# Cross-attention on Trainium2: score products in two row strips, value products in blocks of four

## What is computed

```python
# layer 0: RMS norms on x and ctx; layer 1: biases, boolean mask (all False here), layer norm
q, k, v = x @ Wq.T + bq, ctx @ Wk.T + bk, ctx @ Wv.T + bv        # (8, 100 or 1444, 128)
scores = einsum('bqhd,bkhd->bhqk', heads(q), heads(k)) / sqrt(8)
attn = softmax(scores, axis=-1)
o = einsum('bhqk,bkhd->bqhd', attn, heads(v))
# layer 0, 1: x = norm(x + o @ Wo.T + bo) (layer 0 without the outer norm); layer 3: x = norm(x + o)
# layer 2: the same with causal scores, then gelu(x @ W1.T + b1) @ W2.T + b2 + x
```

## Time and profile before

| | us |
|---|---|
| median of 3 runs | 1240.93 |
| lowest, highest | 1237.69, 1241.09 |
| profiled execution | 1242.44 |
| its span | 1240.6 |
| TensorE busy | 1059.6 (85%) |
| VectorE busy | 857.3 (69%) |
| ScalarE busy | 825.3 (67%) |
| GpSimd busy | 372.6 (30%) |
| mean granted TensorE clock | 0.96 of 2.4 GHz |

### The profile page before, as it was taken

The page is one execution under the profiler, slowest core; times in us unless marked ns, Lnnn a source line. Parts: engine busy times, 40 slices in busy tenths (PEclk is TensorE's granted clock), DMA queues, the critical chain, the costliest instruction groups (busy, mean ns, idle before and its releaser), DMA issues.

```text
span 1240.6 us, 30123 instructions
## 1 busy us (share of the span) xinstructions
PE 1059.6 (85%) x9938; PEld 638.9 (51%) x9938; DVE 857.3 (69%) x1757; ACT 825.3 (67%) x1788; POOL 372.6 (30%) x339
## 2 busy tenths in 40 slices
PE   1469888888998999988998889998999989998886
PEld 0245445445555555655555555565556556565442
DVE  5678678578766766875876657576777858777650
ACT  1237756667776777776777676657677766767565
POOL 6744433344411311330231413232242413323000
PEclk9979999899999999998999999799999999999898
DMA  7212212212221221221232120202021121201100
GB/s 187 62 37 58 61 27 58 58 30 60 65 58 33 73 74 32 72 79 38 58 77 52 39 71 21 55 24 58 22 62 35 48 61 28 61 24 31 35 3 4
DMA packets 57587, 62.92 MB, mean 51 GB/s; under 512 B 16826, under 2 KB 50906, under 8 KB 57302
## 3 DMA queue, kind: packets, MB, share of 16 engines
q1 hardware_dynamic: 57430, 60.89, 19.0%
HBM read 23.63 MB, written 0.41 MB: 19 GB/s over the span
## 4 chain that ended last, share of the span: by engine, by line
PE 58%; DVE 16%; issue 10%; ACT 10%; SPq 3%; DMA 1%; POOL 1%; DVEq 0%; ACTq 0%; POOLq 0%
PE sexp L700 15%; PE acc L719 14%; PE smax L664 12%; DVE mx L1096 7%; ACT probs L965 5%; PE shared L616 3%; PE shared L604 3%; SPq L403 2%; DVE mneg L1102 2%; PE shared L593 2%; PE shared L784 2%; PE smax L676 1%; DVE qs L1083 1%; PE shared L626 1%; SPq L469 1%
## 5 line engine op out<-in xcount | busy, mean ns | idle before, releaser
L965 ACT ACTIVATE probs<-sexp 120x400 f32<-120x400 f32 (+1 forms) x1152 | 558.9, 511 | 237.9 <-PE sexp L700 226.6
L1096 DVE TENSOR_TENSOR mx<-smax,mx 120x400 f16<-120x400 f32 (+1 forms) x1056 | 557.2, 567 | 167.7 <-PE smax L664 161.4
L700 PE MATMUL sexp<-qexp,krep 97*120 97x400 f16 (+1 forms) x1152 | 403.8, 360 | 61.1 <-ACT probs L965 41.8
L664 PE MATMUL smax<-qmax,krep 96*120 96x400 f16 (+1 forms) x1152 | 367.3, 350 | 37.5 <-DVE mx L1096 29.1
L700 PEld LDWEIGHTS sexp<-qexp,krep 97*120 97x120 f16 (+1 forms) x1152 | 152.1, 136 | 216.7 <-ACT probs L965 144.6
L719 PE MATMUL acc<-probs,vx 120*18 120x200 f32 (+1 forms) x4608 | 262.1, 347 | 1.0 <-ACT probs L965 0.9
L664 PEld LDWEIGHTS smax<-qmax,krep 96*120 96x120 f16 (+1 forms) x1152 | 157.6, 138 | 92.6 <-DVE mx L1096 51.3
L488 POOL TENSOR_TENSOR ct<-ctf,ct 128x480 f16<-128x480 f32 (+1 forms) x72 | 82.8, 1151 | 346.2 <-ACT ct L902 346.2
L719 PEld LDWEIGHTS acc<-probs,vx 120*18 120x18 f32 (+1 forms) x4608 | 109.0, 99 | 114.8 <-issue 84.5
L1094 DVE CAST mx<-smax 121x400 f16<-121x400 f32 x96 | 51.3, 570 | 120.3 <-PE smax L664 120.2
L488 POOL TENSOR_TENSOR kp<-kf,kp 128x480 f16<-128x480 f32 (+1 forms) x72 | 79.2, 1106 | 114.6 <-ACT kp L916 114.6
(11 more groups left out here) (133 smaller groups left out, 994.0 us busy)
## 6 DMA issues: line engine op xcount, KB each, us to landing
nat<-in_ctx SPq DMA_DIRECT2D x24, 720.0 KB
krep<-kp SPq DMA_DIRECT2D x576, 30.0 KB, 1.9
krep<-kp SPq DMA_DIRECT2D x288, 30.2 KB, 1.9
qexp<-qmax SPq DMA_DIRECT2D x24, 300.0 KB, 3.4
maskexp<-maskmax SPq DMA_DIRECT2D x8, 281.2 KB, 3.4
anymask<-in_mask SPq DMA_DIRECT2D x1, 1128.1 KB, 6.7
mask<-in_mask SPq DMA_DIRECT2D x8, 141.0 KB
wq<-in_w_qkv SPq DMA_DIRECT2D x1, 768.0 KB
```

The lines of the kernel that those rows point to most:

```text
L664: last = pe.matmul(ps, krep[0:PARTS, u.par, t, c0:c0 + r], qmax[:, u.par, t, :, :].rearrange("p h s -> p (h s)"), start=True, stop=not masks)
L700: last = pe.matmul(ps, krep[:, u.par, t, c0:c0 + r], qexp[:, u.par, t, :, :].rearrange("p h s -> p (h s)"), start=True, stop=not masks)
L965: act.activation(probs[0:r, j % PR, :], sexp[j % SR][0:r, 0:QW], ACT.Exp).then_inc(sem["probs_ready"], 1)
L1096: op = dve.tensor_tensor(dst, src, dst, ALU.max)
```

## The change

Score products. `krep` and the new `qx` have two strips of 64 rows. A strip holds, for its half of the heads, 16 rows of keys three times (48 rows, `KROWS`), then a row of ones that meets the maximum row. A tile is now (chunk, pair of t, strip i) and its score product two products of 48 or 49 rows by 200 columns, a = 0 and 1, into the halves of one bank. Exp and maximum products are issued in turns, and maximum tiles run `LEAD = 13` tiles ahead of the step, so that the maximum tile of a step lies in the other strip than its exp tile; maximum tiles now fill all 48 steps, the first 13 of a unit in the stage before.

Queries. `qmax` and `qexp` become one tile `qx` with three buffers; there is no copy for the exponentials. The maximum row goes out as two DMAs. VectorE's correction of the low part covers all 128 rows.

Keys. `keep_keys` writes `kp` to HBM (3 DMAs a unit), `replicate` reads it back into `krep` in 6 DMAs a group instead of 12.

Value products. `TOGETHER = 2`: blocks of four products, each still over the four column groups.

Order. The maxima are transposed in the shared banks at steps 36 and 37 and `mn` is at 41. Stages are written out with constant semaphore values instead of loops. The two copies of the program behind the flag start at stage 6.

The diff, cut to its core:

```diff
-PARTS = 3 * 32
+PARTS = 128
+STRIP = 64
+KROWS = 48
-TOGETHER = 4
+TOGETHER = 2
 VALUES_AT = [j // TOGETHER * TOGETHER + TOGETHER + 1 for j in range(NSTEP)]
-MAX_AT = [i * 39 // NSTEP for i in range(NSTEP)]
-MT_AT = 39
+LEAD = 13
...
+        def tile_of(j):
+
+            return j // T, j // 2 % 2, j % 2
+
+        def max_tile(s, j):
+
+            u, i = (s.top, j + LEAD) if j + LEAD < NSTEP else (s.prep, j + LEAD - NSTEP)
+            return (u, i) if u is not None else None
...
             while n <= last:
-                b0 = units[n].batch if 0 <= n < len(units) else None
-                if b0 == 1 and n + 3 <= last:
-                    for i in range(2):
-                        await_read(engine, i)
-                    with engine.Fori(1, 4, 2) as b:
-                        enter_loop(n, units, b)
-                        run(stage_of(n, units, b, n), n)
-                        run(stage_of(n + 1, units, b, n), n)
-                        leave_loop(n, units, b)
-                    n += 4
-                else:
-                    run(stage_of(n, units), n)
-                    n += 1
+                run(stage_of(n, units), n)
+                n += 1
...
-        MASK_STAGES = B - 1, 2 * B - 1
+        MASK_STAGES = B - 2, 2 * B - 1
...
+            def keep_keys(u, g):
+
+                _, c0, n, _ = groups()[g]
+                sp.wait_ge(*at("k_lo", u, g + 1))
+                sp.wait_ge(*at(f"krep_in{g}", u, PER[f"krep_in{g}"][u.L] * -1))
+                sp.dma_start(kept[u.par, :, :, c0:c0 + n], kp[:, :, c0:c0 + n]).then_inc(sem[f"k_kept{g}"], 16)
...
-                for t in range(T):
+                for i in range(2):
                     for j, part in enumerate((0, 0, 1)):
-                        sp.dma_start(krep[32 * j:32 * j + 32, u.par, t, c0:c0 + n],
-                                     kp[32 * t:32 * t + 32, part, c0:c0 + n]).then_inc(sem[f"krep_in{g}"], 16)
+                        at_row = STRIP * i + 16 * j
+                        sp.dma_start(krep[at_row:at_row + 16, u.par, :, c0:c0 + n],
+                                     kept[u.par, :, part, c0:c0 + n].rearrange("(t i r) n -> i r t n", t=T, i=2)[i]
+                                     ).then_inc(sem[f"krep_in{g}"], 16)
...
+                    pe.wait_ge(*at("probs_ready", u, j - SR + 1))
+                at_row = STRIP * i
                 ps = sexp[j % SR][0:r, 0:QW]
-                last = pe.matmul(ps, krep[:, u.par, t, c0:c0 + r],
-                                 qexp[:, u.par, t, :, :].rearrange("p h s -> p (h s)"), start=True, stop=not masks)
+                last = pe.matmul(ps[:, 2 * S * a:2 * S * a + 2 * S],
+                                 krep[at_row:at_row + KROWS + 1, u.par, 2 * tp + a, c0:c0 + r],
+                                 qx[at_row:at_row + KROWS + 1, u.third, 2 * tp + a, :, :].rearrange("p f s -> p (f s)"),
+                                 start=(a == 0 or not masks), stop=not masks, skip_group_check=masks)
...
-                for p in range(2):
-                    q, slot = 2 * (t % 2) + p, t // 2
-                    last = pe.matmul(acc[32 * q:32 * q + VW, 2 * S * slot:2 * S * slot + 2 * S],
-                                     vx[0:r, u.par, PAIRS * c + 2 * t + p, :],
-                                     probs[0:r, j % PR, 2 * S * p:2 * S * p + 2 * S],
-                                     start=(c == 0 and slot == 0), stop=(c == NCH - 1), skip_group_check=True)
+                for a in range(2):
+                    q = 2 * a + i
+                    last = pe.matmul(acc[32 * q:32 * q + VW, 2 * S * tp:2 * S * tp + 2 * S],
+                                     vx[0:r, u.par, PAIRS * c + 2 * (2 * tp + a) + i, :],
+                                     probs[0:r, j % PR, 2 * S * a:2 * S * a + 2 * S],
+                                     start=(c == 0 and tp == 0), stop=(c == NCH - 1), skip_group_check=True)
...
             def stage(s, n, masks=False):
                 for j in range(NSTEP):
-                    if s.exp is not None:
-                        exp_scores(s.exp, j, masks and s.exp.L == 1)
-                    for i in range(NSTEP):
-                        if MAX_AT[i] == j and s.top is not None:
-                            max_scores(s.top, i, masks and s.top.L == 1)
+                    m = max_tile(s, j)
+                    for a in range(2):
+                        if s.exp is not None:
+                            exp_product(s.exp, j, a, masks and s.exp.L == 1)
+                        if m is not None:
+                            max_product(*m, a, masks and m[0].L == 1)
...
                         for i in range(3):
-                            act.wait_ge(*at(act, f"krep_in{i}", u, 0))
+                            act.wait_ge(*at(f"k_kept{i}", u, 0))
...
-                dve.tensor_tensor(qs[32:64, :, :], qf[32:64, :, :], qs[32:64, :, :], ALU.subtract
-                                  ).then_inc(sem["q_parts"], 1)
+                dve.scalar_tensor_tensor(out=qs[:, :, :], in0=qs[:, :, :], scalar=headmask[:, 2:3], in1=qf[:, :, :],
+                                         op0=ALU.mult, op1=ALU.add).then_inc(sem["q_parts"], 1)
```

More of the change, by code:

```diff
@@ L244, in build, with at @@
             READ[f"mk{g}"] = ("mask_ready", g + 1)
-        registers = {}
-        def at(engine, name, u, k):
-            per = PER[name][u.L]
-            value = B * sum(PER[name][:u.L]) + per * u.batch + k
-            if u.reg is None or not per:
-                return sem[name], max(value, 0)
-            if engine not in registers:
-                registers[engine] = ([engine.alloc_register(f"count{i}") for i in range(4)], {})
-            counts, products = registers[engine]
-            if per > 1 and (per not in products or products[per][1] is not u.reg):
-                product = products[per][0] if per in products else engine.alloc_register(f"times{per}")
-                engine.reg_mul(product, u.reg, per)
-                products[per] = (product, u.reg)
-            term = products[per][0] if per > 1 else u.reg
-            if value == 0:
-                return sem[name], term
-            counts.append(counts.pop(0))
-            engine.reg_add(counts[-1], term, value)
-            return sem[name], counts[-1]
+        def at(name, u, k):
+            return sem[name], max(B * sum(PER[name][:u.L]) + PER[name][u.L] * u.batch + k, 0)
         def groups():
@@ L320, in build @@
         held = [None, None]
-        def last_uses(s):
-            ends = [(AT["v1"], "v1", s.top), (AT["mk2"], "mk2", s.prep if s.prep.L == 1 else None),
-                    (AT["mn"], "mn", s.top), (AT2["o"], "o2", s.att2)]
-            for _, use, u in sorted((x for x in ends if x[2] is not None), key=lambda x: x[0]):
-                held[bank(use, u)] = (use, u)
         def await_read(pe, i):
@@ L450, in stage @@
                 if s.prep is not None:
+                    for g in range(3):
+                        keep_keys(s.prep, g)
                     replicate(s.prep, 0, s.exp, NSTEP // 3)
@@ L869, in stage @@
                         queries(s.prep)
-                    if s.top is not None and j == MT_AT:
-                        maxima(s.top)
+                    for i in range(2):
+                        if s.top is not None and j == AT[f"mt{i}"]:
+                            maxima(s.top, i)
                     if s.top is not None and j == AT["mn"]:
@@ L1207, in stage @@
                 for j in range(NSTEP):
-                    for i in range(NSTEP):
-                        if MAX_AT[i] == j and s.top is not None:
-                            maximum(s.top, i)
+                    m = max_tile(s, j)
+                    if m is not None:
+                        maximum(*m)
                     if s.post is not None and j == AT["O"] + 1:
@@ L1272, in _ @@
             dve.memset(ones[:, :], 1.0).then_inc(sem["rest_ready"], 1)
-            pipeline(dve, UNITS, stage, first=-2)
+            pipeline(UNITS, stage, first=-2)
 def kernel(**inputs):
```

401 lines of the change are left out of this document (195 added, 206 removed).

## The result

The changed kernel takes 1384.62 us (median of four runs, 1377.46 to 1396.1) against 1241.01 for the kernel before on the same chip: ratio 1.117, interval 1.1083 to 1.1256. It is 12% slower where 1165 us, 6% faster, was forecast. The profiled execution spans 1394.3 us against 1240.6.

What follows compares the result with a forecast made beforehand. TensorE was taken as the bound, with small stalls rather than saturated. Twelve stages -43, eight with layer 2 -11, jumps -16, head -6, tail -1 sum to -77: 1242 to 1165 us; range 1090 to 1280, own range 1120 to 1210.

Steps and rivals of the forecast that it cites:

- rival E: TensorE's clock: with less streamed per us the 1.2 GHz level comes more often, above 1260 us; chance 0.05.
- the stall: Stage time beyond TensorE's demand: from 6.2 us to 3 in layers 0 and 1, 2.5 with layer 2.
- A step: Exp and maximum score products side by side in two strips: 0.19 us a step in place of 0.34.
- B: Rival at the score products: strips do not overlap, a step stays 0.34 us, about 1276 us; chance 0.17.
- Value blocks: Blocks of four at 0.60 us each in place of eight at 0.94: +3.1 us a stage.
- Changes between modes: Switches between strips and full array at shared products: 0.12 us each, 3.7 us a layer 1 stage, 6.4 with layer 2.
- C: Rival at the mode changes: a full drain and load cost 0.21 us each, 1283 us in all; chance 0.13.
- D: Rival on stage length: nearly all stalls go, stages 36.5 and 46.5 us, 1091 us in all; chance 0.15.
- Jumps: Three loop jumps with "issue" gaps and low clock behind them go once loops are written out: -16 us.
- Head: First stages: waits for the second unit's rows and key copies go (-8), larger query weights cost 2: -6 us.
- Tail: Last exp stage +2 us, with no maximum tile to pair; the stage before it gains 3: -1 us.
- Keys through HBM: 36 key copies and a query copy per unit become 3 writes and 18 reads: hidden; uncovered, some 3 us a stage.

Runs made afterwards that it cites:

- before_t2: The kernel before with value blocks of four instead of eight (TOGETHER = 2) and nothing else: 1297.14 us, ratio 1.0432.
- before_flat: The kernel before with its stages written out instead of loops, nothing else: 1225.69 us, ratio 0.9852.
- before_flat_lead: The kernel before with stages written out and maximum tiles in all 48 steps, 13 ahead; whole-array scores and blocks of eight kept: 1193.76 us, ratio 0.9625.
- before_flat_lead_pad: The kernel before, stages written out, maximum tiles 13 ahead, score products over 128 rows, added query rows zero: 1186.54 us, ratio 0.9546.

## Why the prediction was wrong

**The failed step is rival E, the clock, which stands in the sum with nothing.** The prediction put the clock aside with a chance of 0.05 because "In the last exp stage TensorE is busy 24.3 of 30.0 us and the clock is 0.97". That row holds, but it is a row of products over 97 rows of the array, and the argument was made with busy time. The change halved the rows, and no row of before showed a stretch of half-height products. After the change the same stage is the worst of all: 36.1 us at clock 0.50, TensorE busy 97% of it. (That stage was no safe witness anyway: blocks of four alone bring it to 0.53 in before_t2.) The price that E named for the lower clock (a stage of 37 us becomes some 60) was about right: 53.4 us at a mean of 0.63.

What the clock cost: adding rows alone took 403 us of low clock away (660 to 257 in the profiled executions) and 128 us of their span (1394.3 to 1266.8), 0.32 us for each; the medians give 0.33. By that, as an estimate, the remaining 156 us down to the level of before are worth another 49, which puts the change at before's clock near 1219 (1268.5 less 49). The term "clock", 0 in the sum, was then about +177. It holds what the smaller blocks did to the clock as well.

**The second is the stall.** The forecast had 39.8 us for a stage in layers 0 and 1. A straight line through the stages of after (length against time at the lower clock) gives 42.2 at the full clock in layer 0 and 44.1 in layer 1. TensorE's demand was not the mistake: 24 x 0.96 = 23.0, shared work 9.6, and 31 changes of about 0.1 make 35.7, forecast 36.8. So the stall, forecast 3 us, is 6.5 to 8.4, no smaller than before (6.2). Of this the wait for the copy of the result sums is 28.4 / 23 = 1.2 us a stage, a wait that the sum didn't have and that the blocks of four bring. Stages at the full clock are thus 2.4 us (x 7) and 4.3 us (x 5) longer than forecast, +38 in sum; 1165 + 38 + 3.5 for the head is 1207. The paragraph above has 1219 by another road, and 1207 + 177 is 1384. That this meets the measured 1384.62 so closely is luck: the stages with layer 2 lie at the full clock too seldom to be checked, and both roads are estimates.

**Point by point.**

- *A step*, 0.19 forecast: 0.20. B (strips don't overlap) is false: the two products of a pair start within 0.01 us of each other where nothing is waited for.
- *Value blocks*, 0.60 forecast with what surrounds them: 151.03 less 150.94 is 0.09, then 0.47, then 0.04 for the half step behind it: 0.60. (Where the prediction works out the pause of the exp scores it gives such a block 0.34 us; its own 0.80 less 0.34 is 0.46, and the pause 0.8 in place of 0.7.) In the old kernel the smaller blocks cost 56 us, some 75 by the term of 3.1 us a stage.
- *Changes between modes*, 0.12 forecast: 0.09 late start ahead of a block as before, 0.04 more for the first half step (0.13 in place of 0.09). C (changes of 0.21) is false. The rule of the Trainium skill (TensorEngine Tiling (Array Packing), Key Properties) that a change drains the engine agrees with the 0.09, and here it is small.
- *D* (stalls go) is false: nothing like 36.5 us was seen.
- *Jumps*, -16 forecast: -15 (before_flat).
- *Maximum tiles over all 48 steps*, part of the stall's fall: -32 (before_flat to before_flat_lead), so this part of the argument holds. In the kernel after nothing of it is left in the stall.
- *Head*, -6 forecast: 138.2 us after, 140.7 before, -2.5. *Tail*, -1 forecast: the last exp stage alone is 36.1 against 29.9 us, by its clock.
- *Keys through HBM*, hidden forecast. SP's queue in the head of after: start, us of issue.

```profile
35.83 5.26 SPq L348 DMA_DIRECT2D kept<-kp  x3
41.19 8.55 SPq L361 DMA_DIRECT2D krep<-kept  x18
```

  13.8 us where 36 copies took 22.8, and no wait for them stands among TensorE's long ones. It was hidden.
- *The flag*: one "issue" gap is left, at the branch on the mask flag, as forecast.

```profile
PE sexp L661 <- issue: 4.0, 1, 4.0
```

**What the strips are worth.** The kernel after with all rows filled and blocks of eight (1231) and the old kernel with loops written out and the maximum tiles spread (1194) differ by the strips, the road of the keys, the query tile and the filled rows. Even so the strips lose 37 us, at clock 0.916 against 0.964, and 44 us against before_flat_lead_pad, whose rows are filled too. At 0.32 us for each us of low clock (196 against 83 us in the profiled executions) the 37 us are nearly all the clock (36 us), as an estimate. So TensorE's shorter steps bring nothing that shows.

**Open.** What starts each fall of the clock. One row shows it right behind an idle time of 1.06 us (157.53 in the timeline of layer 0; the value block at 157.84 is recorded with 0.83 in place of 0.54), but the runs do not single such waits out. Nor is it shown why smaller blocks cost the clock 0.07 with strips and 0.02 without. Nor did any run vary the number of weight columns in use; the value products (120 rows, 18 columns in each of four column groups) may count for little too; that is a guess.

## What to carry to other kernels

Before a large product is made half as high to run two of them side by side, look at the granted clock: a kernel that sits near the full clock may hold it only by the rows that it uses, and a busy TensorE is no proof of a safe clock. Fill unused rows of the array with zeros on one side; that cost no time in TensorE and gave 0.6% in a kernel at 0.964 and 5 to 8% in one at 0.769. When a change bundles several parts, try those that have nothing to do with its main idea alone: here written-out stages and an even spread of one tile per step brought 3.8%, and the main idea lost it.

## What the runs showed of the hardware that I had not expected

The clock depends on the rows of the array in use. Products over 96, 72 and 48 rows, of the same columns, ran at a clock of 0.960, 0.860 and 0.631; streaming zeros into further rows raised it from 0.769 to 0.839 and 0.880 with strips, and from 0.964 to 0.979 with the whole array. The Trainium skill (TensorEngine Tiling (Array Packing), When to Use Tiling) gives a contraction of 64 rows or fewer as the case for two row tiles. Here two overlapped strips of 48 rows did shorten a step of two 400-column tiles from 0.34 to 0.20 us, and the kernel was 12% slower, 5% with blocks of eight.

A lower clock costs less than its ratio. Over the whole kernel it was 0.32 us for each us at 1.2 GHz, since other engines set part of a stage. Where TensorE alone sets the pace it was 0.42: a block with its two steps is 0.96 us at 2.4 GHz and 1.65 at 1.2, 0.69 more.
